# Output projection of a low-rank layer on one core: pairs of token tiles in a seven-product form

## Chip, cores and metric

One core of one Trainium2 chip. The metric is the device time of one execution in microseconds (us), taken as the median over runs. Everything is float32 in DRAM.

## What is computed

2048 tokens (32 sequences of 64) with 1024 features. A layer with a base weight W and eight gated low-rank experts (A, B, router Wr; the two best experts of each token, softmax of their logits, plus 5.0 on the logit of the sequence's own language) is followed by a layer whose weight is U diag(S) V^T of rank 256, and its result is added to x:

```python
logits = x @ Wr.T + 5.0 * one_hot(language)
gates  = softmax over the top 2 of logits, 0 elsewhere
c      = x @ W.T + 2.0 * sum_e gates_e * (x @ A_e.T) @ B_e.T
out    = x + ((c @ V) * S) @ U.T
```

Since the second layer has rank 256, the kernel never makes c. It makes z = c @ V (256 columns for each token) and then z @ (diag(S) U^T), 256 by 1024.

## The kernel before

**Numbers.** TensorE multiplies in the type fp32r. Each float32 operand is split in two parts: ScalarE copies it to fp32r (the high part, names with `_hi`), and VectorE or GpSimd takes the difference from the original (the low part, `_lo`). A product is then three matmuls, high by high, high by low and low by high (`triple`, L243 to L246). So each thing that TensorE multiplies needs a ScalarE instruction and then a VectorE or GpSimd instruction ahead of it.

**Set-up (about the first 37 us).** TensorE makes P = W^T V (`p_chunk`) into four PSUM banks `fin0` to `fin3`, and from B and V the matrix `bv` (`make_bv`). The right side of the first stage, `proj`, has 392 columns: 128 for the experts' A, 8 for the router, 256 for P. `scale_u` (L430, L500) makes the split of U S, `us_hi` and `us_lo`.

**Token tiles.** There are 16 tiles of 128 tokens. TensorE's order of work for step s (L339) is written out by hand: `project` tile s (8 triples over 392 columns, into bank `pj[s % 2]`); in the midst of it, after the second triple, the transpose of tile s-1's gated expert values h (`transpose_gh`, L289, into bank `gt`), and after the fifth the `mix` of tile s-1 (one triple of 256 columns that adds h times `bv` to z of tile s-1); behind the projection the two transposes of z of tile s-1 (`transpose_z`, L298, into the left half of bank `zt`); then `expand` (L306) of tile s-2: two halves of 512 output columns, each of two triples (z has two blocks of 128 columns), into the next of the four banks `fin`. In step 2 the transpose of h comes later (`gh_at=5`), mix behind the projection and the transposes of z between the two halves. After step 15 the last three tiles are expanded, with the transposes and mix of tile 15 put between (L386 to L397); the last 512 columns are done as two halves of 256.

**What the other engines do in step s, each in its own written order.**

- ScalarE (`step`, L434): the high part of x of tile s+1 (`split_x`, L424, which also waits until the projection of tile s-1 has left its buffer), the high part of h of tile s-1 (L439), the copy of z of tile s-1 out of PSUM (`z_sb`, L441), the high part of the transposed z (L443), and the exponential of the gates of tile s (L446).
- VectorE (`step`, L575): low part of h of tile s-1 (L552); gates of tile s, which are a chain of small instructions: `logit`, `top`, `dtop` (L525, which releases ScalarE's exponential), `top_i`, `chosen` (L528), `rsum`, `pick` (L539), `gate` (L543) and `gh` (L545, which releases the transpose of h); then `residual` (L559) of tile s-2's first half, which adds x to the bank of `fin` and frees it, the low part of z of tile s-1 (L557) and the second `residual`.
- GpSimd (L235): only the low part of x, `xT_lo`, one instruction of 1024 columns for each tile (L237), after the high part.
- SyncE issues all loads and stores of this stage in one queue (L206): transposed x four tiles ahead (`xt_raw`), x six tiles ahead (`x_all`), and the store of a tile once both its `residual` are done.

`chosen`, `pick` and `gate` read two tiles in SBUF each. `logit`, `gh`, `residual` and the low parts of h and z read one tile in PSUM and one in SBUF (`gh` also a column of scalars). `dtop` reads one tile in SBUF.

Of the kernel before, what the change touches and what calls it, by code (L numbers as in the profile page):

```python
# [5 lines left out]
F32 = mybir.dt.float32  # L6
# [10 lines left out]
def adaln_ffn(nc, xt, x, ids, VW, W, AW, B, U, S, out):  # L17
# [27 lines left out]
    with ExitStack() as ctx:  # L45
# [51 lines left out]
        zT_hi = sb("zT_hi", [P, 2, RANK], F32R)  # L97
        zT_lo = sb("zT_lo", [P, 2, RANK], F32R)
# [50 lines left out]
        zt_hi = sem("zt_hi")  # L149
        zt_lo = sem("zt_lo")  # L150
        fin_done = sem("fin_done")
        fin_free = sem("fin_free")

        LAST = TILES - 1
        PIECES = HALF * TILES + 1

        def fin_bank(i):
            return fin[i % FINS]
# [8 lines left out]
        def _(sp):  # L167
# [13 lines left out]
            def store(t):  # L181
                sp.wait_ge(fin_free, HALF * t + HALF)
                sp.dma_start(out_v[t, :, :], x_all[:, t % XR, :]).then_inc(stored[t % XR], 16)

# [21 lines left out]
            for s in range(TILES):  # L206
                if s + XTR < TILES:
                    load_xt(s + XTR)
                if s >= 3 and s - 3 + XR < TILES:
                    load_x(s - 3 + XR)  # L210
                if s >= 2:
                    store(s - 2)
            for n in range(HALF):
                cols = slice(n * BANK, (n + 1) * BANK)
                sp.wait_ge(fin_free, HALF * (LAST - 1) + n + 1)
                sp.dma_start(out_v[LAST - 1, :, cols], x_all[:, (LAST - 1) % XR, cols]).then_inc(stored[(LAST - 1) % XR], 16)
            for n in range(3):
                lo, hi = ((0, BANK), (BANK, BANK + BANK // 2), (BANK + BANK // 2, D))[n]
                sp.wait_ge(fin_free, HALF * LAST + n + 1)
                sp.dma_start(out_v[LAST, :, lo:hi], x_all[:, LAST % XR, lo:hi]).then_inc(stored[LAST % XR], 16)  # L220
# [6 lines left out]
        def _(pool):  # L227
# [7 lines left out]
            for t in range(TILES):  # L235
                pool.wait_ge(xt_hi, t + 1)
                nc.gpsimd.tensor_sub(xT_lo[:, t % 2, :, :], xt_raw[:, t % XTR, :, :],  # L237
                                     xT_hi[:, t % 2, :, :].bitcast(F32)).then_inc(xt_lo, 1)


        @block.tensor
        def _(pe):
# [55 lines left out]
            def transpose_z(t):  # L298
                pe.wait_ge(z_copied, t + 1)
                if t >= 1:  # L300
                    pe.wait_ge(zt_lo, t)
                for m in range(MC):
                    last = nc.tensor.transpose(zt[:, m * P:(m + 1) * P], z_sb[:, m * P:(m + 1) * P], ident[:, :])  # L303
                last.then_inc(zt_done, 1)

            def expand(t, n, parts=range(MC)):  # L306
                i = HALF * t + n
                q = t % 2
                o = slice(n * BANK, (n + 1) * BANK)
                if 0 in parts:  # L310
                    pe.wait_ge(zt_lo, t + 1)
                    if i >= FINS:
                        pe.wait_ge(fin_free, i - FINS + 1)
                for m in parts:
                    zk = slice(m * P, (m + 1) * P)
                    last = triple(fin_bank(i)[:, :], zT_hi[:, q, zk], zT_lo[:, q, zk], us_hi[:, m, o], us_lo[:, m, o],
                                  m == 0, m == MC - 1)
                    if m == MC - 1:
                        last.then_inc(fin_done, 1)

            def expand_end(j):
                i = HALF * LAST + 1 + j
                q = LAST % 2
                o = slice(BANK + j * (BANK // 2), BANK + (j + 1) * (BANK // 2))
                pe.wait_ge(fin_free, i - FINS + 1)
                for m in range(MC):
                    zk = slice(m * P, (m + 1) * P)
                    last = triple(fin_bank(i)[:, 0:BANK // 2], zT_hi[:, q, zk], zT_lo[:, q, zk],
                                  us_hi[:, m, o], us_lo[:, m, o], m == 0, m == MC - 1)
                last.then_inc(fin_done, 1)  # L330
# [8 lines left out]
            def step(s, gh_at=1, mix_at=4, z_after=None):  # L339
# [21 lines left out]
                if s >= 1 and z_after is None:  # L361
                    transpose_z(s - 1)
                if s == 2:
                    pe.wait_ge(us_lo_done, MC)
                if s >= 2 and s < LAST:
                    for n in range(HALF):
                        expand(s - 2, n)
                        if z_after == n:
                            transpose_z(s - 1)
# [12 lines left out]
            step(2, gh_at=5, mix_at=DC - 1, z_after=0)  # L382
# [11 lines left out]
            expand(LAST - 1, 1)  # L394
            expand(LAST, 0)
            for j in range(2):
                expand_end(j)  # L397
# [3 lines left out]
        def _(act):  # L401
# [31 lines left out]

            def step(s):  # L434
                if s >= 1 and s + 1 < TILES:
                    split_x(s + 1)
# [230 lines left out]
```

## Time and profile before

| | us |
|---|---|
| median of 3 runs | 162.8 (162.08, 163.09, 162.80) |
| the profiled execution, its own time | 161.95 |
| its span, from the first to the last instruction | 160.2 |
| TensorE busy in the span | 154.1 (96%) |
| VectorE, ScalarE, GpSimd busy | 81.6, 55.5, 40.4 |

The profile comes from one execution. Its own time lies 0.85 us below the median, and its span 1.75 us below its own time. "Busy" for TensorE is the union of overlapping matmuls: a matmul of 512 columns is shown with about 0.39 us though one starts every 0.23 us. Differences of starts are the measure of what a matmul costs.

### The profile page before, as it was taken

The numbers are of one execution on the slowest core, as the hardware profiler recorded it, in microseconds if no ns is written. First come the engines' busy times: TensorE is split into PE (matmuls) and PEld (weight loads), VectorE is DVE, ScalarE is ACT, GpSimd is POOL, SyncE is SP. The second block draws the span as 40 slices with busy tenths as digits, with TensorE's granted clock in tenths as the row PEclk, the third lists the DMA queues.
The fourth block names the chain that finished last, engine by engine and source line by source line (L and its number), as shares of the span: only waits on it lengthen the run. The fifth ranks groups of instructions, "written<-read, shape, count | busy, mean of one in ns | idle before, by whom it ended". The sixth has DMA issues, their size and how long they took to land.

```text
span 160.2 us, 2469 instructions
## 1 busy us (share of the span) xinstructions
PE 154.1 (96%) x900; PEld 142.4 (89%) x900; DVE 81.6 (51%) x260; ACT 55.5 (35%) x132; POOL 40.4 (25%) x31
## 2 busy tenths in 40 slices
PE   7599999999999999999999999999999999999992
PEld 4499999998998999999998989898989898989882
DVE  0696983455946263535444453536262717081843
ACT  4684881526334323241404041414141414111210
POOL 2000060072354150606060505142323323200000
PEclk9999999999999999999999999999999999999999
DMA  5999999973300859283837474656553430303055
GB/s 176 391 403 406 392 410 408 409 302 125 128 7 0 260 208 314 100 301 119 278 131 262 141 252 158 241 169 224 197 200 131 131 131 0 131 4 131 0 202 191
DMA packets 10522, 32.69 MB, mean 204 GB/s; under 512 B 1424, under 2 KB 1936, under 8 KB 10384
## 3 DMA queue, kind: packets, MB, share of 16 engines
q1 hardware_dynamic: 10224, 31.96, 54.5%
q10 hardware_dynamic: 288, 0.59, 1.0%
q8 instruction: 7, 0.11, 0.3%
q14 instruction: 3, 0.02, 0.1%
HBM read 24.16 MB, written 8.39 MB: 203 GB/s over the span
## 4 chain that ended last, share of the span: by engine, by line
PE 91%; DMA 3%; ACT 2%; DVE 1%; issue 0%; SPq 0%
PE pj L244 15%; PE pj L246 15%; PE pj L245 15%; PE fin L244 14%; PE fin L246 14%; PE fin L245 14%; DMA vw_raw<-in_VW 3%; PE zt L303 2%; PE gt L291 1%; ACT us_hi L431 1%; PE zt L246 1%; PE zt L244 1%; PE zt L245 1%; ACT xT_hi L428 1%; DVE w_lo L487 0%
## 5 line engine op out<-in xcount | busy, mean ns | idle before, releaser
L237 POOL TENSOR_TENSOR xT_lo<-xt_raw,xT_hi 128x1024 fp32r<-128x1024 f32 x16 | 39.3, 2454 | 95.8 <-ACT xT_hi L428 95.8
L244 PE MATMUL pj<-proj_hi,xT_hi 128*128 128x392 f32 x128 | 45.1, 352 | 0.0
L246 PE MATMUL pj<-proj_hi,xT_lo 128*128 128x392 f32 x128 | 43.6, 341 | 0.0
L245 PE MATMUL pj<-proj_lo,xT_hi 128*128 128x392 f32 x128 | 43.4, 339 | 0.0
L244 PE MATMUL fin<-us_hi,zT_hi 128*128 128x512 f32 (+1 forms) x66 | 27.0, 409 | 0.0
L246 PE MATMUL fin<-us_hi,zT_lo 128*128 128x512 f32 (+1 forms) x66 | 25.6, 388 | 0.0
L245 PE MATMUL fin<-us_lo,zT_hi 128*128 128x512 f32 (+1 forms) x66 | 25.6, 388 | 0.0
L244 PEld LDWEIGHTS pj<-proj_hi,xT_hi 128*128 128x128 f32 x128 | 24.0, 188 | 1.2
L245 PEld LDWEIGHTS pj<-proj_lo,xT_hi 128*128 128x128 f32 x128 | 24.1, 188 | 0.6
L246 PEld LDWEIGHTS pj<-proj_hi,xT_lo 128*128 128x128 f32 x128 | 24.0, 188 | 0.0
L520 DVE SCALAR_TENSOR_TENSOR logit<-target,pj 128x8 f32<-128x8 f32 x16 | 2.6, 163 | 40.6 <-PE pj L246 40.6
L565 DVE TENSOR_TENSOR x_all<-fin,x_all 128x512 f32<-128x512 f32 x31 | 21.2, 686 | 2.5 <-PE fin L246 2.5
L244 PE MATMUL fin<-v_hi,w_hi 128*128 128x256 f32 x60 | 17.1, 285 | 1.4 <-DVE w_lo L487 1.4
L245 PE MATMUL fin<-v_lo,w_hi 128*128 128x256 f32 x60 | 17.0, 283 | 0.0
L246 PE MATMUL fin<-v_hi,w_lo 128*128 128x256 f32 x60 | 17.0, 283 | 0.0
L428 ACT CAST xT_hi<-xt_raw 128x1024 fp32r<-128x1024 f32 x16 | 16.6, 1040 | 0.0
L441 ACT COPY z_sb<-pj 128x256 f32<-128x256 f32 x16 | 6.0, 374 | 25.8 <-PE pj L246 25.8
L246 PEld LDWEIGHTS fin<-us_hi,zT_lo 128*128 128x128 f32 x66 | 12.4, 188 | 2.8
L439 ACT CAST ghT_hi<-gt 128x128 fp32r<-128x128 f32 x16 | 4.3, 266 | 30.3 <-PE gt L291 30.3
L244 PEld LDWEIGHTS fin<-us_hi,zT_hi 128*128 128x128 f32 x66 | 12.4, 188 | 2.1
L245 PEld LDWEIGHTS fin<-us_lo,zT_hi 128*128 128x128 f32 x66 | 12.5, 189 | 2.0
L443 ACT CAST zT_hi<-zt 128x256 fp32r<-128x256 f32 x16 | 6.0, 374 | 22.2 <-PE zt L303 22.2
(71 smaller groups left out, 188.8 us busy)
## 6 DMA issues: line engine op xcount, KB each, us to landing
xt_raw<-in_xt SPq DMA_DIRECT2D x16, 512.0 KB, 4.1
x_all<-in_x SPq DMA_DIRECT2D x16, 512.0 KB, 3.6
out<-x_all SPq DMA_DIRECT2D x14, 512.0 KB, 2.9
vw_raw<-in_VW SPq DMA_DIRECT2D x6, 384.0 KB, 6.1
w_raw<-in_W SPq DMA_DIRECT2D x8, 256.0 KB, 9.8
u_raw<-in_U SPq DMA_DIRECT2D x1, 1024.0 KB, 13.0
out<-x_all SPq DMA_DIRECT2D x3, 256.0 KB, 2.0
aw_raw<-in_AW SPq DMA_DIRECT2D x1, 544.0 KB, 8.1
```

Of the source, the lines that this page charges most:

```text
L237: nc.gpsimd.tensor_sub(xT_lo[:, t % 2, :, :], xt_raw[:, t % XTR, :, :], xT_hi[:, t % 2, :, :].bitcast(F32)).then_inc(xt_lo, 1)
L244: nc.tensor.matmul(dst, l_hi, r_hi, start=first, stop=False, skip_group_check=shared)
L245: nc.tensor.matmul(dst, l_hi, r_lo, start=False, stop=False, skip_group_check=shared)
L246: return nc.tensor.matmul(dst, l_lo, r_hi, start=False, stop=last, skip_group_check=shared)
L291: nc.tensor.transpose(gt[:, 0:P], gh[:, :], ident[:, :]).then_inc(gt_done, 1)
L303: last = nc.tensor.transpose(zt[:, m * P:(m + 1) * P], z_sb[:, m * P:(m + 1) * P], ident[:, :])
L428: nc.scalar.copy(xT_hi[:, t % 2, :, :], xt_raw[:, t % XTR, :, :]).then_inc(xt_hi, 1)
L439: nc.scalar.copy(ghT_hi[:, :], gt[:, 0:P]).then_inc(gt_hi, 1)
L441: nc.scalar.copy(z_sb[:, :], pj[(s - 1) % 2][:, Z0:COLS]).then_inc(z_copied, 1)
L443: nc.scalar.copy(zT_hi[:, (s - 1) % 2, :], zt[:, 0:RANK]).then_inc(zt_hi, 1)
L520: nc.vector.scalar_tensor_tensor(logit[:, :], target[:, s, :], LANG_BIAS, pj[q][:, LOG:LOG + E], ALU.mult, ALU.add).then_inc(gate_step, 1)
L565: nc.vector.tensor_add(x_all[:, t % XR, cols], fin_bank(i)[:, :], x_all[:, t % XR, cols]).then_inc(fin_free, 1)
```

## The change

Tiles are taken by pairs: pair p has the tiles 2p and 2p+1. With the two blocks of 128 columns of z of each tile, a pair is a 2 by 2 matrix of 128 by 128 blocks (x11, x12 for tile 2p, x21, x22 for tile 2p+1), and U S is a 2 by 2 matrix of 128 by 512 blocks. Pairs 1 to 6 compute their product by a Strassen (Winograd) form with 7 block products in place of 8. Pairs 0 and 7 are done as before, with 8. What goes with it:

- New left sides: four sums of the blocks of z of a pair (`sums`, VectorE, 128 columns each, two of which read one tile in SBUF and one in PSUM as a difference, one two tiles in SBUF), a ScalarE copy of x22 in front, and one split of all five blocks together (640 columns: ScalarE `split_zb`, VectorE `split_zb`, which reads two tiles in SBUF).
- New right sides, once: four sums of the blocks of U S (`make_y` on ScalarE, 2 x 1024 columns; `make_tsum` on GpSimd, 4 x 512 columns) and their split (`split_t(0)`, `split_t(1)`: 1024 columns each on ScalarE and on VectorE).
- New sums of results for each such pair: `copy_u` (ScalarE, 512 columns out of PSUM), `up(p, 1)` and `up(p, 2)` (VectorE, PSUM and SBUF to SBUF, 512 columns), and three GpSimd additions of 512 columns, SBUF and SBUF to SBUF (`side`), which add these to x before the four `residual` of the pair.
- The order on TensorE: step 2 expands both halves of tile 0, steps 3 and 4 one half of tile 1 each. Step 2p+3 has the first five products of pair p (P1, P6, P7, P5, P2), step 2p+4 the other two (P4, P3), for p from 1 to 5. Pair 6 and pair 7 come after step 15.
- ScalarE makes the high part of x two tiles ahead in step s (s+2; before, s+1), and in the even steps it makes the high part of h in front of it and of the split of z.
- Loads and stores of x go by pairs.

```diff
@@ gpsimd @@
+            for t in range(5):
+                split_x(t)
+            make_tsum()
+            split_x(5)
+            split_x(6)
+            for p in range(1, PAIRS - 1):
+                pool.wait_ge(fin_read, READS * (p - 1) + 1)
+                side(2 * p + 1, 0, 1)
+                side(2 * p, 1, 1)
+                if 2 * p + 5 < TILES:
+                    split_x(2 * p + 5)
+                pool.wait_ge(fin_read, READS * (p - 1) + 3)
+                side(2 * p + 1, 1, 2)
+                if 2 * p + 6 < TILES:
+                    split_x(2 * p + 6)
@@ tensor @@
+            def p1(p):
+                pe.wait_ge(za_lo, p + 1)
+                free_bank(p, 1, 4)
+                product(p, bank_a, 0, *us(0, 0), True, False)
+            def p6(p):
+                pe.wait_ge(zb_lo, p + 1)
+                free_bank(p, 2, 1)
+                product(p, bank_b, 4, *t_of(1), True, True)
...
+            def p2(p):
+                pe.wait_ge(u_copied, p)
+                product(p, bank_a, 1, *us(1, 0), False, True)
+            def p4(p):
+                pe.wait_ge(fin_read, READS * (p - 1) + 2)
+                product(p, bank_c, 2, *t_of(3), False, True)
+            def p3(p):
+                pe.wait_ge(fin_read, READS * (p - 1) + 3)
+                product(p, bank_d, 6, *us(1, 1), False, True)
+            def first_part(p):
+                if p == 1:
+                    pe.wait_ge(tl_done, 2)
+                p1(p)
+                p6(p)
+                p7(p)
+                p5(p)
+                p2(p)
...
-            expand(LAST - 2, 0)
-            expand(LAST - 2, 1, parts=[0])
+            p = PAIRS - 2
+            q = (PAIRS - 1) % 2
+            p1(p)
+            p6(p)
+            p7(p)
+            p5(p)
             transpose_gh(LAST)
-            expand(LAST - 2, 1, parts=[1])
-            expand(LAST - 1, 0, parts=[0])
+            p2(p)
+            p4(p)
             mix(LAST)
-            expand(LAST - 1, 0, parts=[1])
+            p3(p)
             transpose_z(LAST)
@@ scalar @@
             def step(s):
+                copy_z(s - 1)
+                if s % 2 == 1:
+                    split_za((s - 1) // 2)
+                    exp_top(s)
+                    if s >= 5:
+                        copy_u((s - 3) // 2)
+                    if s + 2 < TILES:
+                        split_x(s + 2)
+                    if s < LAST:
+                        split_gh(s)
+                elif s == 2:
+                    exp_top(s)
+                    split_zb_plain(0)
+                    split_x(4)
+                    split_gh(s)
+                    for m in range(MC):
+                        make_y(m)
+                else:
+                    exp_top(s)
+                    copy_x22((s - 2) // 2)
+                    split_gh(s)
+                    split_zb((s - 2) // 2)
+                    if s + 2 < TILES:
+                        split_x(s + 2)
...
+            for s in range(1, TILES):
                 step(s)
+                if s == 3:
+                    split_t(0)
+                if s == 4:
+                    split_t(1)
@@ vector @@
             def step(s):
+                p = (s - 3) // 2
+                if s >= 5 and s % 2 == 1:
+                    split_zb(p)
                 gates_top(s)
                 gates_apply(s)
...
+                elif s == 4:
+                    sums(1)
+                    split_gh(s)
+                    residual_end(3, bank_d, 1, BANK, D)
+                    split_t(0)
+                    split_t(1)
+                elif s == LAST:
+                    up(p, 1)
+                    up(p, 2)
+                elif s % 2 == 1:
+                    up(p, 1)
+                    up(p, 2)
+                    xb1(p)
+                    xa0(p)
+                    split_za(p + 1)
+                    split_gh(s)
+                else:
+                    sums((s - 2) // 2)
+                    split_gh(s)
+                    xb0(p)
+                    xa1(p)
...
+            split_gh(LAST)
+            split_za(PAIRS - 1)
+            xb1(p)
+            xa0(p)
```

`xa0`, `xa1`, `xb0`, `xb1` are the `residual` of the four 512-column quarters of a pair (a: tile 2p, b: tile 2p+1); `fin_read` counts `up`, `up`, `xb1`, `xa0`, `xb0`, `xa1` of each pair.

## Rows read from the trace of the kernel before

**Rows 1.** The page: busy time by engine, and the chain that ended last.
```profile
PE 154.1 (96%) x900; PEld 142.4 (89%) x900; DVE 81.6 (51%) x260; ACT 55.5 (35%) x132; POOL 40.4 (25%) x31
PE 91%; DMA 3%; ACT 2%; DVE 1%; issue 0%; SPq 0%
```

**Rows 2.** Waits of TensorE: engine, tile, line, releaser, us, times, longest.
```profile
PE fin L244 <- DVE w_lo L487: 1.4, 1, 1.4
...
PE pj L244 <- DVE ghT_lo L552: 0.2, 1, 0.2
```

**Rows 3.** Timeline around step 8: start us, us, engine, line, operation.
```profile
86.41 0.23 DVE L525 TENSOR_SCALAR dtop<-top 128x2 f32<-128x2 f32 x1
...
86.88 1.04 ACT L428 CAST xT_hi<-xt_raw 128x1024 fp32r<-128x1024 f32 x1
...
87.47 0.35 DVE L545 SCALAR_TENSOR_TENSOR gh<-pj,rsum,gate 128x128 f32<-128x128 f32 x1
...
87.99 2.41 POOL L237 TENSOR_TENSOR xT_lo<-xt_raw,xT_hi 128x1024 fp32r<-128x1024 f32 x1 [5.36 <-ACT xT_hi L428]
...
88.24 0.39 PE L245 MATMUL fin<-us_lo,zT_hi 128*128 128x512 f32 x1
...
88.47 0.40 PE L246 MATMUL fin<-us_hi,zT_lo 128*128 128x512 f32 x1
...
88.71 0.34 PE L244 MATMUL pj<-proj_hi,xT_hi 128*128 128x392 f32 x1
...
90.08 0.27 ACT L439 CAST ghT_hi<-gt 128x128 fp32r<-128x128 f32 x1 [2.17 <-PE gt L291]
...
91.49 0.28 PE L244 MATMUL pj<-bv_hi,ghT_hi 128*128 128x256 f32 x1
...
93.59 0.48 PE L244 MATMUL fin<-us_hi,zT_hi 128*128 128x512 f32 x1
93.65 0.16 DVE L520 SCALAR_TENSOR_TENSOR logit<-target,pj 128x8 f32<-128x8 f32 x1 [2.98 <-PE pj L246]
```

**Rows 4.** Groups by form: busy us, mean ns of one.
```profile
L565 DVE TENSOR_TENSOR x_all<-fin,x_all 128x512 f32<-128x512 f32 x31 | 21.2, 686 | 2.5 <-PE fin L246 2.5
...
L552 DVE TENSOR_TENSOR ghT_lo<-gt,ghT_hi 128x128 fp32r<-128x128 f32 x16 | 4.7, 292 | 12.1 <-ACT ghT_hi L439 12.1
...
L603 DVE TENSOR_TENSOR b_lo<-b_raw,b_hi 128x1024 fp32r<-128x1024 f32 x1 | 1.2, 1217 | 0.0
...
L413 ACT CAST w_hi<-w_raw 128x512 fp32r<-128x512 f32 x8 | 5.0, 622 | 3.2 <-PE fin L246 3.2
...
L431 ACT ACTIVATE us_hi<-u_raw,s_col 128x1024 fp32r<-128x1024 f32 x2 | 2.3, 1139 | 0.0
```

**Rows 5.** Timeline of steps 2 to 3, the place of the new right sides.
```profile
49.85 0.34 PE L244 MATMUL pj<-proj_hi,xT_hi 128*128 128x392 f32 x1
...
51.23 0.27 ACT L439 CAST ghT_hi<-gt 128x128 fp32r<-128x128 f32 x1 [1.08 <-PE gt L291]
...
54.81 0.16 DVE L520 SCALAR_TENSOR_TENSOR logit<-target,pj 128x8 f32<-128x8 f32 x1 [2.99 <-PE pj L246]
```

**Rows 6.** Timelines: where VectorE and GpSimd run side by side.
```profile
21.30 2.41 POOL L237 TENSOR_TENSOR xT_lo<-xt_raw,xT_hi 128x1024 fp32r<-128x1024 f32 x1 [19.42 <-ACT xT_hi L428]
...
21.77 2.49 DVE L487 TENSOR_TENSOR w_lo<-w_raw,w_hi 128x512 fp32r<-128x512 f32 x1 [0.47 <-ACT w_hi L413]
...
31.45 1.22 DVE L603 TENSOR_TENSOR b_lo<-b_raw,b_hi 128x1024 fp32r<-128x1024 f32 x1
...
31.73 3.19 POOL L237 TENSOR_TENSOR xT_lo<-xt_raw,xT_hi 128x1024 fp32r<-128x1024 f32 x1 [8.02 <-ACT xT_hi L428]
...
34.52 0.43 DVE L525 TENSOR_SCALAR dtop<-top 128x2 f32<-128x2 f32 x1
```

More of the change, by code:

```diff
@@ L148, in adaln_ffn @@
         zt_done = sem("zt_done")
[L149 to L152, printed above, removed]
-        LAST = TILES - 1
-        PIECES = HALF * TILES + 1
-        def fin_bank(i):
-            return fin[i % FINS]
+        x22_copied = sem("x22_copied")
+        sums_done = sem("sums_done")
+        za_hi = sem("za_hi")
+        za_lo = sem("za_lo")
+        zb_hi = sem("zb_hi")
+        zb_lo = sem("zb_lo")
+        y_done = sem("y_done")
+        tsum_done = sem("tsum_done")
+        th_done = sem("th_done")
+        tl_done = sem("tl_done")
+        prod = sem("prod")
+        u_copied = sem("u_copied")
+        fin_read = sem("fin_read")
+        side_add = sem("side_add")
+        end_prod = sem("end_prod")
+        end_read = sem("end_read")
+        LAST = TILES - 1
+        PAIRS = TILES // 2
+        FAST = PAIRS - 2
+        HEAD_PRODS = 2 * HALF
+        PRODS = 7
+        READS = 6
+        ADDS = 3
+        bank_a, bank_b, bank_c, bank_d = fin
         def w_chunk(i):
@@ L208, in _ @@
                     load_xt(s + XTR)
[L209 to L220, printed above, removed]
+                if s >= 6 and s % 2 == 0:
+                    load_x(s)
+                    load_x(s + 1)
+                if s in (4, 5):
+                    store_head(s - 4)
+                if s >= 7 and s % 2 == 1:
+                    store_pair((s - 5) // 2)
+            store_pair(PAIRS - 2)
+            for n in range(5):
+                t, lo, hi = ((LAST - 1, 0, BANK), (LAST - 1, BANK, D), (LAST, 0, BANK),
+                             (LAST, BANK, BANK + BANK // 2), (LAST, BANK + BANK // 2, D))[n]
+                sp.wait_ge(end_read, HEAD_PRODS + n + 1)
+                sp.dma_start(out_v[t, :, lo:hi], x_all[:, t % XR, lo:hi]).then_inc(stored[t % XR], 16)
             for j in range(XR):
@@ L234, in _, with split_x @@
                 nc.gpsimd.memset(iota_e[:, e:e + 1], float(e)).then_inc(const, 1)
-            for t in range(TILES):
+            def split_x(t):
                 pool.wait_ge(xt_hi, t + 1)
@@ L321, in expand_end, with product, us @@
[L321 to L325, printed above, removed]
+            def product(p, dst, x, y_hi, y_lo, first, last):
+                q = p % 2
+                triple(dst[:, :], zh[:, q, x, :], zl[:, q, x, :], y_hi, y_lo, first, last, shared=True).then_inc(prod, 1)
+            def us(m, n):
+                cols = slice(n * BANK, (n + 1) * BANK)
+                return us_hi[:, m, cols], us_lo[:, m, cols]
@@ L364, in step @@
                     pe.wait_ge(us_lo_done, MC)
[L365 to L369, printed above, removed]
+                    pe.wait_ge(za_lo, 1)
+                    expand(0, bank_a, 0, 0, BANK)
+                    transpose_z(1)
+                    expand(0, bank_b, 0, BANK, D)
+                if s == 3:
+                    pe.wait_ge(zb_lo, 1)
+                    expand(0, bank_c, MC, 0, BANK)
+                if s == 4:
+                    expand(0, bank_d, MC, BANK, D)
+                if s >= 5 and s % 2 == 1 and s < LAST:
+                    first_part((s - 3) // 2)
+                if s >= 6 and s % 2 == 0:
+                    second_part((s - 4) // 2)
             pe.wait_ge(const, 1)
@@ L471, in _ @@
             split_x(1)
-            step(0)
+            exp_top(0)
             act.wait_ge(s_load, 16)
@@ new lines, in residual, with xb1, xa0 @@
+            def residual(p, src, after, t, n):
+                cols = slice(n * BANK, (n + 1) * BANK)
+                dve.wait_ge(x_load[t % XR], 16 * (t // XR + 1))
+                dve.wait_ge(prod, PRODS * (p - 1) + after)
+                nc.vector.tensor_add(x_all[:, t % XR, cols], src[:, :], x_all[:, t % XR, cols]).then_inc(fin_read, 1)
+            def xb1(p):
+                residual(p, bank_d, 4, 2 * p + 1, 1)
+            def xa0(p):
+                residual(p, bank_a, 5, 2 * p, 0)
@@ L604, in _ @@
             dve.wait_ge(setup, 2)
-            step(0)
+            gates_top(0)
+            gates_apply(0)
             dve.wait_ge(s_load, 16)
```

261 lines of the change are left out of this document (182 added, 79 removed).

## The prediction, made before the changed kernel was run

> **What bounds the kernel now.** I read the page first: TensorE is busy 96% of the span and carries 91% of the chain that ended last [rows 1]. Then its waits: after the first microseconds it waited once for the low part of w (1.4 us) and once for the low part of h (0.2 us) [rows 2], so nothing in the steps of the token tiles holds it. Then the timeline of one step, to get what a matmul costs and how much room the helpers have. Two matmuls of 512 columns follow each other by 0.23 us (88.24, 88.47) [rows 3]; the 0.39 shown for one is its length in the pipe. Five steps lie between the starts at 49.85 [rows 5] and 88.71 [rows 3], so a step takes 7.77 us. Its projection part takes 4.97 (88.71 to the first product at 93.59, which starts some 0.09 early), which leaves 2.80 for twelve matmuls, 0.2333 each. TensorE is the bound, and time can only be won by giving it less work, as long as its helpers keep up.
>
> I name times in a step by the distance from its first projection matmul. From rows 3: ScalarE's high part of h starts at +1.37 (90.08), the low part may end at +2.64 before the mix (matmul at +2.78) is late; the gates start at +4.94 (93.65); their `dtop` ends 0.76 after that; `gh` starts 1.59 after their first instruction and ends 1.94 after it (86.41 and 87.47, taken back to a start at 85.88), and VectorE goes on at 1.86.
>
> **What is removed.** Six pairs take 21 matmuls of 512 columns in place of 24: 18 x 0.2333 = **-4.20 us**. Projection, mixes, transposes and set-up stay. Odd steps become 4.97 + 15 x 0.2333 = 8.47 us, even ones 4.97 + 6 x 0.2333 = 6.37, steps 3 and 4 6.37. DMA moves the same bytes; x of a pair is asked for in step 2p and first used in step 2p+3, over 14 us later, so the order by pairs costs nothing. ScalarE gains about 0.59 (`copy_u`) + 0.27 (x22) and loses nothing that matters; in the odd step `copy_u` ends near +6.6 and P2 starts at +7.77, so 1 us of cover lies there.
>
> **What is added on VectorE and GpSimd, and their port.** The trace shows something [rows 6] that the old steps never meet, since GpSimd starts only when the gates are through (87.99 against `gh` 87.47 [rows 3]). `w_lo`, two tiles in SBUF, normally 0.69 us, took 2.49 when it started under `xT_lo`, and ended 0.55 after it. `xT_lo` took 3.19 in place of 2.41 when it started under `b_lo`. `dtop`, 2 columns, took 0.43 in place of 0.23 and ended with `xT_lo` (34.95 against 34.92). So the second to start waits for the end of the first. `x_all<-fin` and the other readers of PSUM keep their 0.68 us beside GpSimd. The Trainium skill says the same in "SBUF — State Buffer", section "Who interferes with whom": VectorE with two SBUF inputs, or in a two-port mode, and a GpSimd instruction that reads SBUF hold one port pair in turn, and whoever issues first keeps it for the whole instruction. By that rule `chosen`, `pick` and `gate`, 16 columns and less, each wait too; the trace agrees for large tiles and for `dtop`, and shows no such case for these three. Whether they do is the largest unknown here.
>
> A GpSimd instruction of 512 columns isn't in the trace. It lies between half of 2.41 (1.20) and all of it; I take 1.3, near half, with a fixed share like VectorE's (0.69 for 512 columns, 1.22 for 1024 [rows 4]). The Trainium skill, "GPSIMD Engine Reference", section "Performance versus the Vector engine", gives 4497 ns for 2048 columns; with 2.41 for 1024 that would be an estimate of 1.37.
>
> Step 3 to 4. Step 3 starts at 49.85 in both kernels [rows 5]. ScalarE does the high part of h (51.23 to 51.5) and then `make_y` twice (1.14 each, one every 1.04): done at 53.6. Its copy of z follows and is in time. GpSimd then has four subtractions, 53.65 to about 59.0, and behind them `xT_lo` of tile 5. The gates of tile 3 start at 54.8, inside that. `dtop` wants the port at 55.3 and gets it when the second subtraction ends, about 56.2; 0.17 later `chosen` finds the third one running, until 57.5; `pick` comes at 57.65, just when the fourth could start. If `pick` wins, `gate` waits for the fourth alone and h is there at 59.5. Its transpose was due at 56.22 + 1.06 = 57.28: **+2.3 us** on TensorE. If `pick` loses, `gate` waits for `xT_lo` of tile 5 too, and h is there at 61.8: +4.6. If small instructions go past, the bound is about +0.1, by `dtop` alone. I take 2.3, the middle one.
>
> Step 5. All from large tiles. VectorE after step 4: `sums` end at +1.6, low part of h +1.67, a residual to +2.56, `split_t(0)` +2.5 to +3.7 (like `b_lo`, 1.22 [rows 4]). ScalarE: high part of h, `split_zb` (0.73, between its 512 and 1024 columns), x of tile 6 at +2.25 to +3.3, and `split_t(1)` to +4.2. GpSimd wants to start `xT_lo` of tile 6 at +3.4 and runs until about +6.0. VectorE's `split_t(1)` is ready at +4.2, waits for that, and ends at +7.1. P1 waits for it (`tl_done`), and was due at +4.97: **+2.1 us**. `split_zb(1)` follows (0.8, 640 columns) and is just in time for P6. Without a port in common P1 would start at about +5.6 (+0.6 to 0.7).
>
> The steady pairs. In an odd step VectorE does the low part of h, two residuals and `split_zb` (+3.1 to +3.9). GpSimd's `xT_lo`, ready at +3.4, comes after it and ends at +6.4, over `dtop` (due to end at +5.7): gates 0.6 late. `up`, `up` then end at +8.8, the low part of h is done 0.4 before it is due, and P4, P3, in the next step, are far off. GpSimd's `side`, `side`, `xT_lo`, `side` (1.3 + 1.3 + 2.4 + 1.3) end at +5.9 of the even step, which makes those gates some 0.2 late, and the sums and all behind them the same. With 1.3 for a `side` the delay grows slowly, to 0.8 at step 15; with 1.37 it grows by 0.25 a pair and the last two pairs lose 0.2 to 0.3 each; with 1.20 it stays. TensorE's cost here: 0 (bounds 0 and 0.6).
>
> The end. Behind step 15 there is no projection between `up` and P4. `up` ends at +8.2 plus the delay, P4 is due at +8.55: 9.1 against 8.55, and `xb1`, which frees P3, about 0.2 more. **+0.8 us** (bounds 0 and 1.5). The last expansions and the final store are as before.
>
> **Sum.** -4.20 + 2.3 + 2.1 + 0.8 = +1.0 us on the profiled execution's 161.95, so 162.95. That execution lies 0.85 under the median, so on the median's footing it is 162.8 + 1.0 = 163.8 us: what TensorE gets back is eaten by two stalls in steps 4 and 5 and one in the tail. A measurement of this kernel tells about 1% (1.6 us) from no change.
>
> **Rivals.**
>
> *A. Small instructions pass the port.* `chosen`, `pick` and `gate` don't wait. -4.20 + 0.1 + 2.1 + 0.8 = -1.2: 161.6 us. For it: no row shows these three waiting. Against: `dtop` is as small and did wait.
>
> *B. The port hardly matters.* Only the plain queueing in step 5 remains: -4.20 + 0.7 = -3.5: 159.3 us. For it: TensorE had no waits before and helpers are busy half of the time. Against: the rows of large tiles [rows 6]; it needs GpSimd and VectorE to miss each other in steps 3 and 5.
>
> *C. `pick` loses the port (the one on the slower side).* Place: step 4's transpose of h. Price: 4.6 in place of 2.3, so +3.3: 166.1 us. It decides by less than 0.1 us, at 57.6: if GpSimd's fourth subtraction starts before `pick`, `gate` also waits for the 2.41 us of `xT_lo`. The change is slower than before from a stall of 1.3 us in step 4 on, the rest as forecast.
>
> *D. `xT_lo` comes in front of `split_zb` in the odd steps.* VectorE is there at +3.1, GpSimd at +3.4. If two residuals cost 0.3 more than their 0.60 each, the order turns: `split_zb` ends at +6.7 and P6, due at +5.67, stalls 1.1, in five steps. -4.20 + 2.3 + 2.1 + 5.5 = +5.7: 168.5 us. Against it: margin 0.3, and both sides shift together with the sums.
>
> **How the numbers follow.** Forecast 0.33, A 0.24, B 0.15, C 0.20, D 0.08. Its own range for the forecast is 162.6 to 165.2. Faster by over 1% (under 161.2): B, nearly half of A, a little of the forecast: 0.28. Slower by over 1% (over 164.4): C, D and a quarter of the forecast: 0.36. Within 1%: 0.36. The range 159.2 to 166.8 holds most of B and C and leaves out D and the edges, under 2 in 10.
>
> **What would show it.** In the profile after: 18 fewer product matmuls of 512 columns, each still 0.2333 after the last. Step 4: TensorE waiting 2.3 us for `gh` or for what follows it, `chosen` or `gate` shown with over 1 us for 16 columns. Step 5: TensorE waiting 2.1 us for the low part of the new right sides, that VectorE instruction with nearly 3 us in place of 1.2. Odd steps: `dtop` with over 0.5 us and no wait on TensorE; `split_zb` in front of `xT_lo`. End: under 1 us of waiting for `up`. I am wrong if the gates' small instructions keep 0.16 us under a running GpSimd (A), if a steady step shows TensorE waiting (D), or if GpSimd's 512 columns take much more than 1.4 us.

## The result and the profile after

The changed kernel took 165.34 us (median of 4 runs, 163.61 to 166.03) against 162.44 us for the kernel before: ratio 1.0158, 95% interval 1.0085 to 1.0230. It is slower, by 2.9 us between the medians and 2.6 between the means. (Medians and ranges are of all executions; ratios and intervals compare means without the few executions over 1.5% above their kernel's fastest, a slower state that comes with every kernel now and then.) 163.8 had been forecast on a base of 162.8 (+1.0), in a range of 159.2 to 166.8. The profiled execution has a span of 163.5 us against 160.2, so +3.3 is what the two traces have to explain.

The page of the changed kernel, beside [rows 1]: busy time, the granted clock in forty slices (in tenths of full speed), and the chain that ended last; below it the clock line of the kernel before.

```profile
PE 154.5 (94%) x882; PEld 143.5 (88%) x882; DVE 105.5 (65%) x298; ACT 65.3 (40%) x148; POOL 69.0 (42%) x53
...
PEclk9999999999999977996999999999999999999998
...
PE 87%; DVE 5%; ACT 3%; DMA 2%; issue 1%; DVEq 0%; ACTq 0%
```
```profile
PEclk9999999999999999999999999999999999999999
```

TensorE has 18 matmuls fewer and is not less busy. VectorE now holds 5% of the chain. The clock line, flat before, has two dents, in slices 15 and 16 and in slice 19, which are the times of steps 4 and 5. (The last digit, 8, belongs to the time behind TensorE's last matmul.)

TensorE's waits in the changed kernel, beside [rows 2]:

```profile
PE fin L305 <- DVE v_lo L755: 1.9, 1, 1.9
PE gt L352 <- DVE gh L744: 1.8, 1, 1.8
...
PE pj L305 <- DVE ghT_lo L751: 0.2, 1, 0.2
```

Two new waits behind the set-up, of 1.83 and 1.94 us, are all there is. (Names follow the memory: `vw_raw` now holds the sums, `v_lo` the low parts of the new right sides, `w_hi` and `w_lo` those of z.)

**Step 4.** VectorE and GpSimd of the changed kernel in step 3:

```profile
55.30 0.89 DVE L724 TENSOR_SCALAR dtop<-top 128x2 f32<-128x2 f32 x1
...
56.36 1.08 DVE L727 TENSOR_TENSOR chosen<-iota_e,top_i 128x16 f32<-128x16 f32 x1
...
57.48 0.18 DVE L738 TENSOR_TENSOR pick<-chosen,etop 128x16 f32<-128x16 f32 x1
57.69 1.11 DVE L742 TENSOR_TENSOR gate<-pick 128x8 f32<-128x8 f32 x1
58.84 0.35 DVE L744 SCALAR_TENSOR_TENSOR gh<-pj,rsum,gate 128x128 f32<-128x128 f32 x1
```
```profile
53.63 1.29 POOL L273 TENSOR_TENSOR vw_raw<-vw_raw 128x512 f32<-128x512 f32 x1 [1.18 <-ACT vw_raw L562]
54.88 1.29 POOL L274 TENSOR_TENSOR vw_raw<-vw_raw 128x512 f32<-128x512 f32 x1
56.12 1.29 POOL L276 TENSOR_TENSOR vw_raw<-vw_raw 128x512 f32<-128x512 f32 x1
57.49 1.29 POOL L278 TENSOR_TENSOR vw_raw<-vw_raw 128x512 f32<-128x512 f32 x1
58.75 2.38 POOL L268 TENSOR_TENSOR xT_lo<-xt_raw,xT_hi 128x1024 fp32r<-128x1024 f32 x1
```

Each of `dtop`, `chosen` and `gate` ends as a GpSimd subtraction ends: 56.19 and 56.17, 57.44 and 57.41, 58.80 and 58.78. `chosen` spends 1.08 us on 16 columns. `pick` slips through: it starts at 57.48 and the fourth subtraction at 57.49. So rival C was missed by 0.01 us of start time in this execution; `gate` would else have stood behind `xT_lo` too.

**Step 5.** The low part of the second two right sides waits for `xT_lo` of tile 6:

```profile
68.63 1.22 DVE L755 TENSOR_TENSOR v_lo<-vw_raw,v_hi 128x1024 fp32r<-128x1024 f32 x1
70.42 2.75 DVE L755 TENSOR_TENSOR v_lo<-vw_raw,v_hi 128x1024 fp32r<-128x1024 f32 x1 [0.57 <-ACT v_hi L566]
```
```profile
69.51 2.57 POOL L268 TENSOR_TENSOR xT_lo<-xt_raw,xT_hi 128x1024 fp32r<-128x1024 f32 x1 [8.39 <-ACT xT_hi L555]
```

The same instruction takes 1.22 us with the port free and 2.75 behind GpSimd.

**What the forecast lacked.** TensorE's matmuls right behind each wait:

```profile
59.25 0.33 PE L352 MATMUL gt<-ident,gh 128*128 128x128 f32 x1 [1.83 <-DVE gh L744]
...
60.25 0.53 PE L305 MATMUL pj<-proj_hi,xT_hi 128*128 128x392 f32 x1
60.58 0.53 PE L306 MATMUL pj<-proj_lo,xT_hi 128*128 128x392 f32 x1
...
74.24 0.63 PE L307 MATMUL fin<-us_hi,w_lo 128*128 128x512 f32 x1
74.66 0.63 PE L305 MATMUL fin<-v_hi,w_hi 128*128 128x512 f32 x1
```

They follow each other by 0.33 us for 392 columns and 0.42 for 512, against 0.18 and 0.23. A view of stretches gives the clock (columns: stretch, length, busy us and count of PE, PEld, DVE, ACT, POOL, granted clock, DMA share, GB/s):

```profile
60.00:62.00 2.00, 2.00 (x8) 2.00 (x7) 0.32 (x2) 0.83 (x1) 1.12 (x1) 0.50 0.00 0
62.50:72.50 10.00, 8.78 (x50) 8.17 (x49) 6.71 (x18) 4.32 (x10) 2.57 (x1) 0.98 0.25 98
74.00:76.00 2.00, 2.00 (x7) 1.52 (x6) 1.47 (x9) 1.40 (x4) 0.00 (x0) 0.50 0.95 383
```

A granted clock of 0.50 is the 1.2 GHz level. So the clock fell within 0.4 us of TensorE's return from each wait of under 2 us, and stayed there for about 3 us (59.6 to 63.0 and 73.2 to 76.6).

From the starts of the steps in both traces:

| | before | after | difference |
|---|---|---|---|
| start of step 3 | 49.85 | 49.83 | 0.0 |
| step 4 | 7.78 | 9.97 | 6.36 without a stall, so 1.83 idle + 1.78 behind it |
| step 5 | 7.76 | 12.16 | 8.40 without one, so 1.94 + 1.82 |
| steps 3 to 14, together | 93.22 | 93.91 | -6.68 of matmuls, +3.61, +3.76 |
| from step 15 to TensorE's last matmul | 14.17 | 16.31 | +2.14, for 9 matmuls more |
| from there to the end of the span | 2.93 | 3.41 | +0.48 |

The matmuls save 6.68 - 2.14 = 4.54 us, the stalls cost 7.37, the end 0.48: +3.3.

### The profile page after: what moved, and what is told of

It reads as the page before. It is cut to its first block, busy times and chain, and to the rows that moved or that the text cites. A ratio compares the mean times of both kernels' runs of the same rounds, so it can differ in the third digit from the quotient of the medians.

```text
span 163.5 us, 2552 instructions
## 1 busy us (share of the span) xinstructions
PE 154.5 (94%) x882; PEld 143.5 (88%) x882; DVE 105.5 (65%) x298; ACT 65.3 (40%) x148; POOL 69.0 (42%) x53
## 3 DMA queue, kind: packets, MB, share of 16 engines
HBM read 24.16 MB, written 8.39 MB: 199 GB/s over the span
## 4 chain that ended last, share of the span: by engine, by line
PE 87%; DVE 5%; ACT 3%; DMA 2%; issue 1%; DVEq 0%; ACTq 0%
PE pj L305 14%; PE pj L307 14%; PE pj L306 14%; PE fin L305 13%; PE fin L306 13%; PE fin L307 13%; PE zt L370 2%; DMA vw_raw<-in_VW 2%; DVE v_lo L755 2%; ACT xT_hi L555 1%; PE gt L352 1%; PE fin L320 1%; ACT us_hi L558 1%; DVE gate L742 1%; DVE chosen L727 1%
## 5 line engine op out<-in xcount | busy, mean ns | idle before, releaser
L283 POOL TENSOR_TENSOR x_all<-x_all,vw_raw 128x512 f32<-128x512 f32 x18 | 23.0, 1292 | 20.6 <-DVE vw_raw L791 20.6
L305 PE MATMUL fin<-v_hi,w_hi 128*128 128x256 f32 (+1 forms) x84 | 27.6, 329 | 0.0
L306 PE MATMUL fin<-v_lo,w_hi 128*128 128x256 f32 (+1 forms) x84 | 26.9, 320 | 0.0
L307 PE MATMUL fin<-v_hi,w_lo 128*128 128x256 f32 (+1 forms) x84 | 26.7, 318 | 0.0
L307 PEld LDWEIGHTS fin<-v_hi,w_lo 128*128 128x128 f32 x84 | 16.5, 196 | 1.1
L305 PEld LDWEIGHTS fin<-v_hi,w_hi 128*128 128x128 f32 x84 | 16.5, 197 | 1.0
L306 PEld LDWEIGHTS fin<-v_lo,w_hi 128*128 128x128 f32 x84 | 16.6, 198 | 0.9
L305 PE MATMUL fin<-us_hi,w_hi 128*128 128x512 f32 (+1 forms) x36 | 15.0, 417 | 1.9 <-DVE v_lo L755 1.9
L307 PE MATMUL fin<-us_hi,w_lo 128*128 128x512 f32 (+1 forms) x36 | 13.9, 387 | 0.0
L306 PE MATMUL fin<-us_lo,w_hi 128*128 128x512 f32 (+1 forms) x36 | 13.9, 387 | 0.0
```

The lines of the kernel that those rows point to most:

```text
L283: nc.gpsimd.tensor_add(x_all[:, t % XR, cols], x_all[:, t % XR, cols], ups[:, j, :]).then_inc(side_add, 1)
L305: nc.tensor.matmul(dst, l_hi, r_hi, start=first, stop=False, skip_group_check=shared)
L306: nc.tensor.matmul(dst, l_hi, r_lo, start=False, stop=False, skip_group_check=shared)
L307: return nc.tensor.matmul(dst, l_lo, r_hi, start=False, stop=last, skip_group_check=shared)
```

## Experiments

The theory going in: the port costs two waits, and each wait is charged twice, once as idle time and once as a stretch at the lower clock. The rivals: the clock falls by the load, by itself or by the place; and the waits hide further limits. The first four experiments ran on one chip and the other four on another; the kernel before has a median of 162.41 us on the first and 162.33 on the second.

### One stall at a time

**e1_early_sums.** The sums of the right sides are made in gaps between gate chains.

```diff
@@ gpsimd
-            for t in range(5):
+            for t in range(4):
                 split_x(t)
-            make_tsum()
+            tsum_first()
+            split_x(4)
+            tsum_middle()
+            tsum_last()
@@ scalar, step
                 copy_z(s - 1)
+                if s == 1:
+                    make_y(0)
...
                     if s < LAST:
                         split_gh(s)
+                    if s == 1:
+                        make_y(1)
...
-                    for m in range(MC):
-                        make_y(m)
```

`tsum_first` waits for `gh` of tile 2 (`gh_done` 3) and does one subtraction, `tsum_middle` two, and `tsum_last` waits for `gh` of tile 3 and does the fourth.

> The right-side sums of the changed kernel are made earlier and in the gaps between two gate chains (make_y in steps 1 and 2; GpSimd's four subtractions at about 48.7, 52.5, 53.7 and, behind gh of tile 3, 56.8). Nothing else is changed. Theory (one port, and the clock after each wait): chosen and gate of tile 3 go back to about 0.17 us, step 4 takes 6.4 us in place of 9.97, step 5 stays at about 12.2 with its 1.9 us wait and slow matmuls; the span falls by 3.6 us from 163.5 to about 159.9. Rival (the clock falls by itself at this place, not because TensorE waited): only the wait of 1.8 us goes, and 0.327 us for each projection matmul remains in step 4; about 161.7.

161.82 us (160.14 to 162.84), ratio to the kernel of before 0.9925 (0.9866 to 0.9985). Step 4 takes 6.36 us, step 5 12.18; the span is 159.8, and 159.9 was expected. TensorE's wait in step 5 is untouched:

```profile
PE fin L314 <- DVE v_lo L766: 1.9, 1, 1.9
```

The slow matmuls of step 4 went with the wait, though the step, its place and the load after it stayed. The rival's 161.7 is out.

**e2_t_early.** Only the order of the splits of the right sides is changed.

```diff
@@ scalar
                 if s == 3:
                     split_t(0)
-                if s == 4:
                     split_t(1)
@@ vector, step 3
                     split_za(1)
                     split_gh(s)
+                    split_t(0)
+                    split_t(1)
@@ vector, step 4
                     residual_end(3, bank_d, 1, BANK, D)
-                    split_t(0)
-                    split_t(1)
```

> Only the split of the new right sides is moved: ScalarE makes both high parts after step 3, VectorE both low parts in front of the gates of tile 4, where it idles in the changed kernel. Theory: step 4 keeps its 9.97 us, step 5 falls from 12.16 to about 8.4 (the wait of 1.94 us and the slow matmuls behind it both go), span about 159.8. Rival (step 5 is late for another reason, the sums of z or the gates): step 5 stays over 10 us.

160.82 us (159.95 to 162.06), ratio 0.9904 (0.9842 to 0.9967). Step 4 takes 9.94, step 5 8.39. The span is 160.3; TensorE's start-up was 0.8 later in this execution (step 0 starts at 30.24 against 29.43), which more than makes up the difference from 159.8.

The four executions of e2 lie in two groups: 162.06 and 161.64 us at a mean clock of 0.987, 159.95 and 160.01 at 0.998. That is 1.87 us between the groups, near the 1.78 that the changed kernel's trace shows behind this wait. The changed kernel does the same: three executions at 0.975 or 0.976 with 165.24 to 166.03 us, one at 0.987 with 163.61. Of the kernels with one such wait, e1_early_sums has the lower clock in two of four executions, e5_write_only in eight of ten, e7_plain_wait in five of six. So the slow stretch comes in most executions, not in all. The wait itself stays: the two executions of e2 at 0.998 are still 1.5 us above the 158.52 of e3_both, which has no wait. Most of the spread of the changed kernel's times comes from the slow stretches; not all of any spread does, since e1_early_sums has its longest time, 162.84 us, at a mean clock of 1.00.

**e3_both.** Both moves; VectorE's share of the two splits is arranged for steps without stalls.

```diff
@@ vector, step
-                if s >= 5 and s % 2 == 1:
+                if s >= 7 and s % 2 == 1:
                     split_zb(p)
@@ vector, step 3
                     split_gh(s)
+                    split_t(0)
@@ vector, step 4
                     sums(1)
                     split_gh(s)
+                    split_t(1)
+                    split_zb(1)
                     residual_end(3, bank_d, 1, BANK, D)
-                    split_t(0)
-                    split_t(1)
```

> Both moves together. Sums as in e1_early_sums; ScalarE makes both high parts after step 3, VectorE the first low part behind step 3 and the second in step 5 directly in front of split_zb(1), both ahead of GpSimd's xT_lo of tile 6, and the residual that frees bank d after them. Theory: no wait of TensorE over 0.3 us after step 1, granted clock 1.00, steps 4 and 5 at 6.4 and 8.4; the span is that of before minus 4.5 plus 0.5 for the last stores, 156.2, and the time about 158.3: faster than before by 2.5 to 3%. Rival (steps 4 and 5 only hide a later limit, GpSimd's or VectorE's growing load): the waits come back in steps 6 to 15 and the span stays above 158.

158.52 us (157.69 to 158.95), ratio 0.9751 (0.9709 to 0.9793): 2.5% faster than before. The span is 157.1 and not 156.2, since the start-up was 1.2 later here (step 0 at 30.61). With it goes a longer slow stretch at the very start: the first matmuls of 256 columns follow each other by 0.21 us until 10.2 us, in the changed kernel's trace until 8.3, in that of the kernel before they come at 0.12 from 5 us on. Steps 4 and 5 take 6.36 and 8.40, all later ones 6.33 to 6.36 and 8.37 to 8.40. Its page and its waits:

```profile
PEclk9999999999999999999999999999999999999999
```
```profile
PE fin L498 <- POOL zeros L258: 1.0, 1, 1.0
PE fin L329 <- ACT w_hi L541: 0.7, 1, 0.7
PE fin L314 <- DVE w_lo L696: 0.3, 1, 0.3
PE pj L314 <- DVE ghT_lo L761: 0.2, 1, 0.2
```

Nothing of TensorE's waiting is left behind step 1, and the rival (further limits behind the two stalls) is out.

### Is it the idle time that lowers the clock?

**e4_fill.** TensorE multiplies zeros while it waits.

```diff
+            def fill(dst, n):
+                for _ in range(n):
+                    nc.tensor.matmul(dst[:, :].rearrange("p (c n) -> p c n", c=CPB), zeros[:, :],
+                                     zeros[:, :].rearrange("p (o n) -> p o n", o=1).to_broadcast([P, CPB, P]),
+                                     start=True, stop=True)
@@ step
+                    if s == 4 and k == gh_at:
+                        fill(bank_d, 8)
                     if s >= 1 and k == gh_at:
                         transpose_gh(s - 1)
...
+                if s == 5:
+                    pe.wait_ge(end_read, 1)
+                    fill(bank_a, 9)
```

> The changed kernel with matmuls of zeros into a free bank where TensorE waited: 8 of 512 columns in front of the transpose of h in step 4, 9 in front of P1 in step 5. Their results are overwritten. The waits as such stay (1.8 and 1.9 us), only TensorE isn't idle in them. Theory (the idle time is what lowers the granted clock): clock 1.00 in steps 4 and 5, the projection's matmuls at 0.18 and the products at 0.233 us, steps 4 and 5 about 8.2 and 10.4 in place of 9.97 and 12.16, span near 160. Rival (the clock falls from the load on the other engines or by itself): pitches of 0.33 and 0.43 stay and the span is 163.5 or more.

162.39 us (161.81 to 162.93), ratio 0.9994 (0.9957 to 1.0032): 3 us less than the changed kernel, with 17 matmuls more. All four executions have a mean clock of 0.997 to 1.00, against 0.975 to 0.987 in the changed kernel. Steps 4 and 5 take 8.43 and 10.68 (8.2 and 10.4 were expected). The stretches that hold the former stalls:

```profile
57.50:63.00 5.50, 5.48 (x30) 4.80 (x30) 3.02 (x8) 1.79 (x4) 3.83 (x3) 1.00 0.11 17
69.00:75.00 6.00, 6.00 (x29) 4.72 (x28) 5.57 (x13) 2.41 (x7) 1.82 (x1) 1.00 0.58 220
```
```profile
59.52 0.33 PE L352 MATMUL gt<-ident,gh 128*128 128x128 f32 x1
...
60.04 0.34 PE L307 MATMUL pj<-proj_hi,xT_lo 128*128 128x392 f32 x1
60.22 0.34 PE L305 MATMUL pj<-proj_hi,xT_hi 128*128 128x392 f32 x1
```

The work behind each wait runs at clock 1.00 and a pitch of 0.18 us, with nearly the same load on the other engines.

This run also splits the cost of a stall. With the clock at 1.00 the two stalls cost 8.43 - 6.36 = 2.07 and 10.68 - 8.40 = 2.28 us (0.1 of the latter can be the ninth matmul of zeros: P1 starts 2.18 late in the changed kernel). The lower clock makes the rest of the changed kernel's 3.61 and 3.76: about 1.5 each (1.54 and 1.48). So of the 1.78 and 1.82 behind the idle time, 0.2 to 0.3 isn't the clock. What follows an idle TensorE starts later than the idle time says, since matmuls overlap (one of 392 columns is shown with 0.34 us and the next starts after 0.18): in step 4 the projection's matmul behind the wait starts at +3.15 in the changed kernel and at +1.09 in e1_early_sums, 2.06 later, for 1.83 of idle time.

**e7_plain_wait.** The kernel of before, with a wait put into step 8 and nothing of the change.

```diff
@@ gpsimd, behind split of tile 8
+                if t == HOLD:
+                    pool.wait_ge(pj_done, HOLD)
+                    for i in range(HOLD_N):
+                        if i:
+                            pool.wait_ge(held, i)
+                        nc.gpsimd.memset(scratch[:, :], 0.0).then_inc(held, 1)
@@ tensor, step
+                    if s == HOLD and k == gh_at:
+                        pe.wait_ge(held, HOLD_N)
```

> The kernel of before with one artificial wait: in step 8 the transpose of h waits until GpSimd has done twelve memsets of 512 columns one after the other, which start when the projection of tile 7 is done; TensorE should idle some 1.5 to 3 us. Nothing of the change is in it. Theory (TensorE's idle time is followed by a stretch at the lower clock, in most executions but not in all): step 8 is longer than 7.77 by the wait and in most executions by about 1.8 us more, at matmul pitches of 0.33 for 392 columns; the executions fall in two groups 1.8 us apart, told by the mean clock (0.987 against 1.00). Rival (the lower clock comes from the changed kernel's load on VectorE and GpSimd): the clock stays 1.00 and the time rises by the wait alone.

166.93 us (166.13 to 167.56), ratio 1.0297 (1.0249 to 1.0345).

```profile
92.58 0.33 PE L301 MATMUL gt<-ident,gh 128*128 128x128 f32 x1 [2.97 <-POOL scratch L248]
...
93.28 0.53 PE L256 MATMUL pj<-proj_hi,xT_lo 128*128 128x392 f32 x1
93.60 0.53 PE L254 MATMUL pj<-proj_hi,xT_hi 128*128 128x392 f32 x1
```
```profile
93.00:96.00 3.00, 3.00 (x12) 3.00 (x11) 0.29 (x1) 0.21 (x1) 1.85 (x1) 0.50 0.61 213
```

Step 8 takes 12.50 us in place of 7.77: 2.97 of waiting and 1.76 more, with the clock at 0.50. Five of six executions show a mean clock of 0.989 or 0.990 (166.60 to 167.56 us), one 0.998 (166.13). The last is only 0.5 under the nearest of the others, so the clear gap of 1.8 that was expected between the groups isn't there, and one execution can't settle it. But the lower clock follows a bare wait in the plain kernel. It needs neither the place nor the load of the change.

### What of GpSimd holds VectorE up?

**e5_write_only.** The four sums of the right sides are left out, and memsets take their time on GpSimd; four of the seven products are then of zeros.

```diff
-                nc.gpsimd.tensor_sub(tsum[:, 0, :], y[:, 0, BANK:], y[:, 0, 0:BANK]).then_inc(tsum_done, 1)
...
+                for j in (0, 2, 1, 3):
+                    nc.gpsimd.memset(tsum[:, j, :], 0.0).then_inc(memset_done, 1)
+                    pool.wait_ge(memset_done, (0, 2, 1, 3).index(j) + 1)
+                    nc.gpsimd.memset(tsum[:, j, :], 0.0).then_inc(tsum_done, 1)
```

> The changed kernel with GpSimd's four subtractions of the right-side sums replaced by eight memsets of 512 columns, two for each sum: the sums are left out (zeros), so four of the seven products are of zeros. GpSimd is then about as busy in step 3 (some 4.8 us from 53.6 on), but reads nothing in SBUF. Theory (VectorE waits for the port because it reads two SBUF tiles while GpSimd reads one): chosen, pick and gate of tile 3 keep 0.15 to 0.18 us under a running memset, h is in time, step 4 takes 6.4 us; step 5 keeps its wait of 1.9 us. dtop may still wait for one memset (0.5 us). Rival (any GpSimd instruction holds VectorE up): chosen and gate show 0.4 us and more, and step 4 stays late by about the length of the memsets in its way.

161.98 us (159.68 to 162.74), ratio 0.9949 (0.9903 to 0.9994). Step 4 takes 6.36, step 5 12.19.

```profile
55.77 0.50 DVE L723 TENSOR_SCALAR dtop<-top 128x2 f32<-128x2 f32 x1
...
56.37 0.18 DVE L726 TENSOR_TENSOR chosen<-iota_e,top_i 128x16 f32<-128x16 f32 x1
...
56.72 0.15 DVE L737 TENSOR_TENSOR pick<-chosen,etop 128x16 f32<-128x16 f32 x1
56.91 0.17 DVE L741 TENSOR_TENSOR gate<-pick 128x8 f32<-128x8 f32 x1
```
```profile
55.73 0.53 POOL L277 MEMSET vw_raw<- 128x512 f32 x1
56.19 0.55 POOL L275 MEMSET vw_raw<- 128x512 f32 x1
56.80 0.53 POOL L277 MEMSET vw_raw<- 128x512 f32 x1
```

`chosen` runs from 56.37 to 56.55 inside a memset (56.19 to 56.74), and `gate` from 56.91 to 57.08 inside the next, both at full speed; beside a subtraction they waited. `dtop` still waits, 0.50 us. This is the split that "SBUF — State Buffer" of the Trainium skill, "Who interferes with whom", makes: a VectorE instruction with two SBUF inputs contends with a GpSimd instruction that reads SBUF and not with one that only writes it. The rows of `chosen` and `gate` agree with both halves. The same section says that a VectorE instruction in a two-port mode, which `tensor_scalar` can enter, contends with GpSimd. That `dtop` waits for memset and subtraction fits this; that it runs in such a mode, no row shows.

### The order that the change chose

**e8_x_first.** e3_both, with ScalarE's high part of x in the even steps back in front of h's.

```diff
                     copy_x22((s - 2) // 2)
+                    if s + 2 < TILES:
+                        split_x(s + 2)
                     split_gh(s)
                     split_zb((s - 2) // 2)
-                    if s + 2 < TILES:
-                        split_x(s + 2)
```

> e3_both, with one part of the change undone: in the even steps ScalarE makes the high part of x two tiles ahead in front of h's high part and the split of z, not behind them. GpSimd's xT_lo then starts about 7.4 us into the even step and is over 3.4 us into the odd one, just over split_zb's start at 3.1, and away from dtop. Theory: dtop of the odd steps falls from about 0.75 to 0.23 us, split_zb rises from 0.81 to at most 1.2, and since neither held TensorE, the time stays that of e3_both within 0.3 us. Rival (the order matters: the high part of h comes late behind x): TensorE waits for h's low part before the mix in odd steps, some tenths of a us each, and the time rises by 1 to 2 us.

A miss. 164.75 us (164.69 to 165.13), ratio 1.0169 (1.0116 to 1.0223): 6.2 us more than e3_both from the place of one line. `dtop` of the odd steps is back at 0.23 as expected, and `split_zb` keeps 0.81. `xT_lo` starts 7.6 us behind the start of step 8 (at 88.72), where it was expected (7.4). What I had not followed is what VectorE does then: behind the gates of an even tile come the sums of z. VectorE and GpSimd there:

```profile
96.20 0.29 DVE L783 TENSOR_TENSOR zs<-zs,zt 128x128 f32<-128x128 f32 x1
96.52 2.30 DVE L785 TENSOR_TENSOR zs<-zs 128x128 f32<-128x128 f32 x1
98.75 0.28 DVE L786 TENSOR_TENSOR zs<-zt,zs 128x128 f32<-128x128 f32 x1
98.95 0.28 DVE L761 TENSOR_TENSOR ghT_lo<-gt,ghT_hi 128x128 fp32r<-128x128 f32 x1
```
```profile
96.29 2.39 POOL L268 TENSOR_TENSOR xT_lo<-xt_raw,xT_hi 128x1024 fp32r<-128x1024 f32 x1 [2.27 <-ACT xT_hi L564]
```

Of the four sums of z, one alone reads two SBUF tiles, and it stands behind `xT_lo` for 2.30 us in place of 0.29. The low part of h is queued behind it, and TensorE waits for that in five odd steps:

```profile
PE pj L314 <- DVE ghT_lo L761: 5.4, 6, 1.2
```

The rival's result (a wait for h's low part, 1.2 and 0.9 us in turn) came about by the theory's mechanism: ScalarE's high part of h starts at +1.37, not late at all. The five waits are 1.20, 0.89, 1.25, 0.89 and 0.89 us, and the clock stays 1.00 behind every one. The five steps take 6.4 us more than 8.40 each would, the waits 5.1: at the full clock too, a wait costs some 0.26 us beyond its idle time.

The set-up of this execution has a longer wait, and the clock stays 1.00 and the pitch 0.12 us for 256 columns behind it:

```profile
8.16 0.39 PE L314 MATMUL fin<-v_hi,w_hi 128*128 128x256 f32 x1 [1.79 <-DVE w_lo L696]
8.38 0.28 PE L315 MATMUL fin<-v_lo,w_hi 128*128 128x256 f32 x1
```

1.79 us without the lower clock and 1.83 with it: the length of a wait alone doesn't tell whether the clock falls, and no run here shows what does.

### The last stores

**e6_quarters.** e3_both, with pair 6 stored in four quarters.

```diff
-            store_pair(PAIRS - 2)
+            p = PAIRS - 2
+            r = READS * (p - 1)
+            for t, n, need, adds in ((2 * p, 0, r + 4, 0), (2 * p + 1, 1, r + 4, ADDS * p), (2 * p + 1, 0, r + 5, ADDS * p),
+                                     (2 * p, 1, r + 6, ADDS * p)):
+                sp.wait_ge(fin_read, need)
+                if adds:
+                    sp.wait_ge(side_add, adds)
+                sp.dma_start(out_v[t, :, n * BANK:(n + 1) * BANK],
+                             x_all[:, t % XR, n * BANK:(n + 1) * BANK]).then_inc(stored[t % XR], 16)
```

> e3_both, with pair 6 stored in four quarters of 256 KB, each as soon as it is ready, in place of two stores of 512 KB after the last quarter. In the profiles the last store ends 2.96 us after TensorE's last matmul before the change and 3.4 us after it with the change. Theory (the two large stores stand in the way of the last five): that falls back to about 3.0, span 156.7 in place of 157.1, time 0.2 to 0.4 us less. Rival (the five small stores alone set it): no change.

158.31 us (157.88 to 159.95), ratio 0.9798 (0.9728 to 0.9867), and the interval holds e3_both's 0.9751. From TensorE's last matmul (152.76) to the end of the span (156.10) it is 3.34 us, against 3.38 in e3_both. (The span is 1.0 shorter than e3_both's by the start-up, with step 0 at 29.49.) The two large stores are not what makes the end 0.4 to 0.5 longer; its cause stays open.

## Why the forecast came out as it did, step by step

**Products.** -4.20 was forecast for 18 matmuls; the starts give -4.5. Even steps are 6.36 as said, odd ones 8.40 to 8.42 against 8.47 (in part of the seven products the pitch is 0.227 in place of 0.233; why, no run shows).

**The port.** The likeliest case of "Step 3 to 4" happened: three small instructions waiting, `pick` slipping through, `gh` ready at 59.2 for 59.5. These forecasts are of late starts, so they compare with the stalls at the full clock in e4_fill: 2.3 forecast (its own times, 59.5 and 57.28, give 2.2), found 2.07, of which TensorE was idle 1.83. "Step 5": forecast 2.1, found 2.28, idle 1.94. GpSimd's 512 columns take 1.29, taken as 1.3. Rivals A and B fall with `chosen` and `gate`; C is close by and didn't happen; D didn't either (`split_zb` has 0.81 us in every odd step and stands in front of `xT_lo` from step 7 on). D's sum, +5.7, also leaves out the 0.8 of the end that the forecast's has.

**The steady pairs.** Forecast 0, found 0. `dtop` is 0.70 to 0.87 in the odd steps 7 to 13 and 0.34 to 0.49 in the even ones that GpSimd's last addition reaches. The delay doesn't grow.

**The end.** +0.8 was forecast, for gates that come late to step 15. Found about 0 (16.31 us against 14.17 + 9 x 0.233 = 16.27). The step that failed: "to 0.8 at step 15". There is no `xT_lo` in front of step 15's gates, since the last tile's runs in step 14 (139.52 to 141.91), so `dtop` has 0.23 us there and nothing is late. In return the stretch from TensorE's last matmul to the end of the span is 0.5 longer, which I had put at nothing ("The last expansions and the final store are as before").

**The clock.** The term that was missing altogether. I priced a stall as its waiting time: "-4.20 + 2.3 + 2.1 + 0.8". Each of the two also brought about 1.5 us (1.54 and 1.48) of matmuls at 1.2 GHz in the profiled execution. With the measured stalls and without this term the sum would be -4.54 + 2.07 + 2.28 + 0.48 = +0.3; with its 3.0, +3.3. It turned "no change" into "slower". The base had no row that showed it: its waits are of 0.2 us in the token tiles and at most 1.4 in the set-up, and the matmuls of 256 columns behind that one come at 0.12 us, as before it.

**How near the number came.** 165.34 lies above the forecast's own range (162.6 to 165.2). It lies inside the whole range only because that was stretched to hold rival C, which didn't happen. And the miss would have been larger but for luck: the missing 3.0 us of the clock and 0.5 of the end were in part covered by the 0.8 of the end that didn't come and 0.3 more saved by the matmuls.

## What to carry to other kernels

Work moved to GpSimd is not free of VectorE: list each VectorE instruction with two SBUF inputs, however small, and each `tensor_scalar` on SBUF, and see which GpSimd instruction can be running when it starts; the small ones in a chain of waits cost up to one whole GpSimd instruction each. A wait of about 2 us put on a busy TensorE cost its length, some 0.3 us of late starts and, in most executions, about 1.5 us more of matmuls at 1.2 GHz, so a saving of some matmuls is worth only as much as the order around it stays without stalls. Here the same products gave +1.6% with two collisions and -2.5% with none, by moving small work into gaps.

## What was not expected of the hardware

- Waits of 1.83, 1.94 and 2.97 us were each followed by about 3 us at a granted clock of 0.50, and the steps grew by 1.78, 1.82 and 1.76 us beyond the wait. Five waits of 0.9 to 1.25 us in e8_x_first left it at 1.00, and so did one of 1.79 us in the same kernel's set-up.
- The lower clock is not certain: in e2_t_early two executions of four had it, 1.87 us above the other two.
- `dtop`, two columns wide, waits even for a memset of GpSimd (0.50 us in place of 0.23); `chosen`, 16 columns and two inputs, doesn't (0.18), but waits 1.08 us for a subtraction.
